# Routed experts on 131 tiles of chosen token rows in whole fp32 words, with the weights resident on chip and rows moved by indirect transfers

## The reference

```
x = x + xattn(layernorm(x), ctx, ctx)              # causal, 16 heads of 16
h = layernorm(x)                                   # (1600, 256)
scores = sigmoid(h @ gate_w.T)                     # (1600, 32)
sc     = scores + gate_bias
# 8 groups of 4 experts; the 4 groups with the best sum of their top two;
# in those the 8 best experts of sc; weights = scores of the 8, normalised, * 2.5
routed = einsum('tei,ehi->th', silu(h @ w_gate) * (h @ w_up) * combine, w_down)   # 32 experts, inner size 128
shared = (silu(h @ sh_gate.T) * (h @ sh_up.T)) @ sh_down.T                        # two more of size 128
out = x + routed + shared
```

## Time and profile before

| what | value |
|---|---|
| time, median of 3 runs | 690.34 us (689.27 to 690.46) |
| span of the profiled execution, first to last instruction | 687.6 us |
| TensorE busy, weight loads busy | 625.4 us, 569.0 us |
| VectorE, ScalarE, GpSimd busy | 559.5, 271.4, 249.4 us |
| granted TensorE clock, mean | 0.975 |
| moved by DMA | 61.66 MB, mean 90 GB/s |

### The profile page before, as it was taken

How to read it: one execution, slowest core, us unless ns; L and a number is a source line. 1 busy time by engine, 2 the same in 40 slices (tenths; PEclk the granted TensorE clock), 3 DMA queues, 4 the chain that set the end, 5 groups by cost and what they waited for, 6 DMA issues and landing times.

```text
span 687.6 us, 13004 instructions
## 1 busy us (share of the span) xinstructions
PE 625.4 (91%) x4232; PEld 569.0 (83%) x4232; DVE 559.5 (81%) x942; ACT 271.4 (39%) x590; POOL 249.4 (36%) x222
## 2 busy tenths in 40 slices
PE   3897999997589999999999999999999999999996
PEld 3885666664489898999999899999999999999995
DVE  5967999994748888888888888888888888888885
ACT  3444665652123333333333333333333333333331
POOL 6530334344013333333333333333333333333332
PEclk9999999998779999999999999999999999999998
DMA  6210000000123343433334343444343433333341
GB/s 192 80 59 1 2 2 3 2 2 0 49 74 94 98 133 97 122 111 113 120 101 131 95 125 109 131 120 125 102 131 94 130 104 119 115 102 132 95 123 49
DMA packets 33373, 61.66 MB, mean 90 GB/s; under 512 B 4008, under 2 KB 14768, under 8 KB 33348
## 3 DMA queue, kind: packets, MB, share of 16 engines
q1 hardware_dynamic: 33348, 61.31, 29.6%
HBM read 59.44 MB, written 1.86 MB: 89 GB/s over the span
## 4 chain that ended last, share of the span: by engine, by line
PE 76%; DVE 16%; issue 5%; ACT 1%; DMA 1%; POOL 0%; SPq 0%; DVEq 0%
PE ps L647 47%; PE ps L813 24%; DVE prob L498 4%; DVE rden L519 3%; DVE nm L489 2%; PE ps L834 2%; DVE st L509 1%; DVE xn L445 1%; DMA cst<-consts 1%; DVE ot L521 1%; DVE x_all L507 1%; PE ps L737 1%; PE ps L700 0%; PE ps L710 0%; PE ps L696 0%
## 5 line engine op out<-in xcount | busy, mean ns | idle before, releaser
L302 POOL TENSOR_TENSOR act<-act,cw 128x400 f32<-128x400 f32 x136 | 178.8, 1315 | 328.5 <-DVE act L595 328.5
L647 PE MATMUL ps<-h_hi_all,w_hi 128*128 128x400 f32 x544 | 189.0, 347 | 4.9 <-DVE w_lo L544 4.9
L393 ACT ACTIVATE act<-ps 128x400 f32<-128x400 f32 x136 | 68.5, 504 | 311.6 <-PE ps L647 311.6
L647 PE MATMUL ps<-h_lo_all,w_hi 128*128 128x400 f32 x544 | 188.9, 347 | 0.0
L647 PE MATMUL ps<-h_hi_all,w_lo 128*128 128x400 f32 x544 | 188.6, 347 | 0.0
L592 DVE SCALAR_TENSOR_TENSOR act<-act,ps 128x400 f32<-128x400 f32 x136 | 77.7, 571 | 83.5 <-ACT act L393 83.5
L813 PE MATMUL ps<-a_hi,w_hi 128*128 128x400 f32 x272 | 99.2, 365 | 19.5 <-issue 17.0
L647 PEld LDWEIGHTS ps<-h_hi_all,w_hi 128*128 128x128 f32 x544 | 103.2, 190 | 5.0 <-issue 5.0
L647 PEld LDWEIGHTS ps<-h_lo_all,w_hi 128*128 128x128 f32 x544 | 103.3, 190 | 0.0
L647 PEld LDWEIGHTS ps<-h_hi_all,w_lo 128*128 128x128 f32 x544 | 103.2, 190 | 0.0
L544 DVE TENSOR_TENSOR w_lo<-w_raw,w_hi 128x512 fp32r<-128x512 f32 x68 | 102.9, 1513 | 0.0
(11 more groups left out here) (118 smaller groups left out, 664.7 us busy)
## 6 DMA issues: line engine op xcount, KB each, us to landing
cw<-combine_rows SPq DMA_DIRECT2D x68, 400.0 KB, 4.0
w_raw<-w_exp SPq DMA_DIRECT2D x68, 256.0 KB, 3.9
w_raw<-w_exp SPq DMA_DIRECT2D x68, 128.0 KB, 2.0
x_all<-x SPq DMA_DIRECT2D x4, 400.0 KB
ctx_f<-ctx_t SPq DMA_DIRECT2D x4, 400.0 KB, 3.7
out_t<-y_out SPq DMA_DIRECT2D x8, 200.0 KB, 2.0
wa<-w_attn SPq DMA_DIRECT2D x4, 256.0 KB, 6.1
cst<-consts SPq DMA_DIRECT2D x1, 266.0 KB, 5.7
```

The lines of the kernel that those rows point to most:

```text
L302: pool.tensor_tensor(act[:, s, :], act[:, s, :], cw[:, (s // 2) % 2, (s % 2) * TG:(s % 2 + 1) * TG], ALU.mult).then_inc(weighted, 1)
L393: a.activation(act[:, s, :], ps[:, 4 + 2 * (s % 2), 0:TG], ACT.Tanh, scale=0.5).then_inc(tanh_e, 1)
L647: last = t.matmul(out, w, m, start=(i == 0), stop=(i == n - 1))
```

## The change

The routed experts are computed only for the rows that chose them. What is new, part by part:

- **Routing moves into the attention loop.** `route(p)` for two batches at a time runs on VectorE from the sixth turn of the loop on. Matmuls with a triangular matrix (`count`) count the rows that chose each expert so far, and `places` makes from it a row number in a DRAM table `chosen_rows`, in which every expert has 2048 places. The split of the normed rows into two parts goes away; the logits are plain fp32 matmuls, batch by batch.
- **Sends.** For each batch GpSimd issues 8 indirect transfers (`send`, L355): the r-th takes the batch's 100 records of 289 words (256 features, the row's number, 32 combine weights) to the places of each row's r-th expert; 128 transfers in all. 32 transfers of SyncE write 128 empty records behind each expert's last one (L274).
- **Weights resident.** All 32 experts' weights (12.6 MB) are loaded once into `w_all`: 9 experts early, 6 after the projections, 17 after the last `values`. The two shared experts are computed over all rows with plain fp32 matmuls (`shared_gate_up`, `shared_product`) and added to `x_all`, which starts the first of three sum tables in DRAM.
- **Tiles.** A table of 131 tiles of 128 rows (the most there can be: 12800 chosen rows plus 32 partly filled tiles) says for each its place and its expert. For each tile SyncE loads two registers and issues two transfers, the rows and their column of combine weights (L287 to L290); TensorE turns the rows (L946), loads a register with the place of the weights (L950), makes two fp32 matmuls for gate and up together (L955), turns the activations (L963) and makes one for down (L969), each 128 rows by 256 columns; ScalarE makes two copies and a tanh, VectorE three operations, GpSimd one indirect transfer that adds the 128 result rows in DRAM to one of the three sum tables by row number (L372). A tile's transfer waits until that of three tiles before has landed (`landed`).
- **End.** The three sum tables are fetched in four blocks, added on VectorE, turned on TensorE, copied and stored.

```diff
+NT = (T * TOPK + NE * (P - 1)) // P
...
+EARLY = 9
+MIDDLE = 6
+NSUM = 3
+NROW = 12
+NOUT = 5
...
+            def experts_load(first_one, end, arrived):
+                sp.dma_start(w_all[:, first_one:end, :], w_exp[2 + first_one:2 + end].rearrange("e p n -> p e n")).then_inc(arrived, 16)
+
...
+            sp.wait_ge(q_ready, KC * NG)
+            experts_load(EARLY, EARLY + MIDDLE, w_middle)
+            sp.wait_ge(pv_psum, NB)
+            for e in range(EARLY + MIDDLE, NE, 4):
+                experts_load(e, min(e + 4, NE), w_late)
...
+            sum_start(0)
+            sp.wait_ge(pads_at, 1)
+            for e in range(NE):
+                at = sp.value_load(pads[0:1, e:e + 1], min_val=0, max_val=PAD_ROWS - CAP + T)
+                sp.dma_start(recs[bass.ds(at, P), :], pad_rec[:]).then_inc(pads_out, 16)
...
+            sp.wait_ge(rows_out, 16 * NB * TOPK)
+            for i in range(NT):
+                b = i % NROW
+                if i >= NROW:
+                    n = (i - NROW) % NSUM
+                    sp.wait_ge(landed[n], times_landed(n, i - NROW + 1))
+                at = sp.value_load(table[0:1, 0, i:i + 1], min_val=0, max_val=PAD_ROWS)
+                e = sp.value_load(table[0:1, 1, i:i + 1], min_val=0, max_val=NE - 1)
+                sp.dma_start(rows[:, b, :], recs[bass.ds(at, P), 0:COMB]).then_inc(row_in[b], 16)
+                sp.dma_start(weight[:, b:b + 1], recs[bass.ds(at, P), bass.ds(e + COMB, 1)],
+                             allow_slow_non_contiguous=True).then_inc(row_in[b], 16)
...
+            for q, (j0, j1) in enumerate(BLOCKS):
+                for n in range(NSUM):
+                    sp.dma_start(fetched(n)[:, j0 * D:j1 * D].rearrange("p (j d) -> p j d", d=D),
+                                 sums[n][j0 * P:j1 * P, :].rearrange("(j p) d -> p j d", p=P)).then_inc(part_in[q], 16)
...
-                pool.tensor_copy(h_hi_all[:, :, batch_cols(B)], h_rows[:, B % 2]).then_inc(h_hi_ready, 1)
-                pool.wait_ge(h_hi_ready, B + 1)
-                pool.tensor_tensor(h_lo_all[:, :, batch_cols(B)], h_rows[:, B % 2], f(h_hi_all[:, :, batch_cols(B)]),
-                                   ALU.subtract).then_inc(h_lo_ready, 1)
...
+            def send(B):
...
+                pool.wait_ge(h1_ready, B + 1)
+                pool.wait_ge(comb_ready, B // 2 + 1)
+                pool.wait_ge(dest_ready, B // 2 + 1)
+                for r in range(TOPK):
+                    pool.indirect_dma_start(out=recs, out_offset=bass.IndirectOffsetOnAxis(ap=dest[:, B, r:r + 1], axis=0),
+                                            in_=rec[:, B, :], in_offset=None).then_inc(rows_out, 16)
...
-            def weigh(N, s, E, new_expert):
-                if new_expert:
-                    pool.wait_ge(cw_in[(s // 2) % 2], 16 * E)
-                pool.wait_ge(gated, N + 1)
-                pool.tensor_tensor(act[:, s, :], act[:, s, :], cw[:, (s // 2) % 2, (s % 2) * TG:(s % 2 + 1) * TG],
-                                   ALU.mult).then_inc(weighted, 1)
...
+                if B >= 5:
+                    send(B - 5)
+            for B in range(NB - 5, NB):
+                send(B)
...
+            for i in range(NT):
+                n = i % NSUM
+                pool.wait_ge(o_ready, i + 1)
+                if i >= NSUM:
+                    pool.wait_ge(landed[n], times_landed(n, i))
+                pool.indirect_dma_start(
+                    out=sums[n], out_offset=bass.IndirectOffsetOnAxis(ap=rows[:, i % NROW, TOKEN:TOKEN + 1].bitcast(U32), axis=0),
+                    in_=out_rows[:, i % NOUT, :], in_offset=None, compute_op=ALU.add).then_inc(landed[n], 16)
...
+            def rows_in(i):
...
+                a.activation(hx[:, i % 3, :], ps[:, i % 2, 0:D], ACT.Copy).then_inc(hx_ready, 1)
...
+            def gate(i):
...
+                a.activation(th[:, i % 2, :], ps[:, 2 + i % 2, 0:FI], ACT.Tanh, scale=0.5).then_inc(t_tanh, 1)
...
+            def acts_in(i):
...
+                a.activation(ax[:, i % 2, :], ps[:, 4 + i % 2, 0:P], ACT.Copy).then_inc(ax_ready, 1)
...
-            def split_gu(count, slot):
-                v.wait_ge(gu_hi, count)
-                v.tensor_tensor(w_lo[:, slot, 0:2 * D], w_raw[:, slot, 0:2 * D], f(w_hi[:, slot, 0:2 * D]),
-                                ALU.subtract).then_inc(gu_lo, 1)
...
+            def route(p):
+                two = slice(2 * p, 2 * p + 2)
+                v.wait_ge(tanh_ready, 2 * p + 2)
...
+                for b in range(2 * p, 2 * p + 2):
+                    then(v.tensor_tensor(so_far[:, b + 1, :], so_far[:, b, :], mask_e[:, b, :], ALU.add))
+                v.scalar_tensor_tensor(taken[:], rt[:, two, :], 1.0, mask_e[:, two, :], ALU.add, ALU.mult).then_inc(mask_ready, 1)
...
+            def places(p):
+                two = slice(2 * p, 2 * p + 2)
+                v.wait_ge(place_psum, p + 1)
+                then(v.tensor_tensor(place[:], ps[0:S, 6 if late_count(p) else 3, TG:TG + 2 * NE].rearrange("p (b e) -> p b e", e=NE), mask_e[:, two, :], ALU.mult))
+                then(*[v.max(first[:, b, :], place[:, b, :]) for b in range(2)])
+                v.tensor_scalar(dest[:, two, :], first[:], -1.0, None, ALU.add).then_inc(dest_ready, 1)
...
+            def gate(i):
+                n = i % 2
+                v.wait_ge(t_tanh, i + 1)
+                v.scalar_tensor_tensor(opened_t[:, n, :], th[:, n, :], 1.0, ps[:, 2 + n, 0:FI], ALU.add, ALU.mult).then_inc(t_open, 1)
+                v.wait_ge(t_open, i + 1)
+                if i >= 2:
+                    v.wait_ge(ax_psum, i - 1)
+                v.scalar_tensor_tensor(gated_t[:, n, :], opened_t[:, n, :], weight[:, i % NROW:i % NROW + 1], ps[:, 2 + n, FI:2 * FI],
+                                       ALU.mult, ALU.mult).then_inc(t_gated, 1)
+
+            def result(i):
+                v.wait_ge(t_down, i + 1)
+                if i >= NOUT:
+                    n = (i - NOUT) % NSUM
+                    v.wait_ge(landed[n], times_landed(n, i - NOUT + 1))
+                v.tensor_copy(out_rows[:, i % NOUT, :], ps[:, 6 + i % 2, 0:D]).then_inc(o_ready, 1)
+
+            for i in range(NT + 2):
...
-                for part_of in range(2):
-                    w = lambda a, k: a[:, slot, (2 * part_of + k) * P:(2 * part_of + k + 1) * P]
-                    last = product(ps[:, 4 + 2 * (s % 2) + part_of, 0:TG],
-                                   [(w(w_hi, k), w(w_lo, k), h_hi_all[:, k, col:col + TG], h_lo_all[:, k, col:col + TG])
-                                    for k in range(KC)])
-                last.then_inc(gu_psum, 1)
...
+            def weights(i):
+                off = place_of[i]
+                return w_all[:].rearrange("p e n -> p (e n)")[:, bass.ds(off, W)].rearrange("p (a n) -> p a n", n=P)
+
+            def rows_turned(i):
+                t.wait_ge(row_in[i % NROW], 32 * (i // NROW + 1))
+                if i >= 2:
+                    t.wait_ge(hx_ready, i - 1)
+                for k in range(KC):
+                    last = t.transpose(ps[:, i % 2, k * P:(k + 1) * P], rows[:, i % NROW, k * P:(k + 1) * P], ident)
+                last.then_inc(hx_psum, 1)
+
+            def gate_up(i):
+                place_of[i] = t.value_load(table[0:1, 2, i:i + 1], min_val=0, max_val=(NE - 1) * W)
+                t.wait_ge(hx_ready, i + 1)
+                if i >= 2:
+                    t.wait_ge(t_gated, i - 1)
+                for k in range(KC):
+                    last = t.matmul(ps[:, 2 + i % 2, 0:D].rearrange("p (a n) -> p a n", n=P), hx[:, i % 3, k * P:(k + 1) * P],
+                                    weights(i)[:, k:2 * KC:2, :], start=(k == 0), stop=(k == KC - 1))
+                last.then_inc(t_gu, 1)
+
+            def acts_turned(i):
+                t.wait_ge(t_gated, i + 1)
+                if i >= 2:
+                    t.wait_ge(ax_ready, i - 1)
+                t.transpose(ps[:, 4 + i % 2, 0:P], gated_t[:, i % 2, :], ident).then_inc(ax_psum, 1)
+
+            def down(i):
+                t.wait_ge(ax_ready, i + 1)
+                if i >= 2:
+                    t.wait_ge(o_ready, i - 1)
+                t.matmul(ps[:, 6 + i % 2, 0:D].rearrange("p (a n) -> p a n", n=P), ax[:, i % 2, :],
+                         weights(i)[:, 2 * KC:3 * KC, :], start=True, stop=True).then_inc(t_down, 1)
+
+            t.wait_ge(table_ready, 1)
+            t.wait_ge(sh_gated, 2 * NG)
+            t.wait_ge(sh_added, 2 * NG)
...
+            for i in range(NT + 2):
+                if i < NT:
+                    gate_up(i)
+                if i >= 2:
+                    down(i - 2)
+                if 1 <= i <= NT:
+                    acts_turned(i - 1)
+                if i + 2 < NT:
+                    rows_turned(i + 2)```

```

(5 more changed lines are left out.)

750 lines of the change are left out of this document (404 added, 346 removed).

## The result

The changed kernel takes **664.51 us** (median of 4 runs, 662.17 to 666.83) beside 690.40 us of the kernel before on the same chip (4 runs, 689.27 to 691.44). The ratio is 0.9627, with a 95% interval of 0.9600 to 0.9654: faster by 3.7%. Forecast were 639 us, with 570 to 770 as the range.

The account below looks back on a forecast made before the run. The prediction took GpSimd's sends to set the tile loop's start and TensorE to pace the tiles: 287 + 321 + 7 + 21 = 636 us of span, plus 2.7 gives 639 us; range 570 to 770.

Parts of the forecast that it names:

- First send: In attention: GpSimd's first indirect transfer of records was to begin at about 111 us.
- q: GpSimd's price for issuing one indirect transfer, taken as 1.2 us, between bounds of 0.56 and 2.84.
- SyncE waits for the last record, loads, fetches: 4 us.: Between the last send and the tile loop: SyncE's wait, register loads and fetch were to take 4 us.
- the 287 of the forecast: Start of the tile loop, forecast at 287 us; a start outside 260 to 310 would make the prediction wrong.
- Attention at 11.4 us a batch, set by GpSimd.: Attention under the sends: GpSimd's eight sends and a norm, 11.4 us a batch, set the pace against VectorE's 9.4.
- The longest is TensorE: 2.45 us a tile.: Tile loop: TensorE's 1.85 us plus a 0.60 register load sets the pace, 131 tiles in 321 us.
- Rival 2: Tile loop: slower register loads make SyncE the pace, 3.55 us a tile and 783 us in all; chance 0.10.
- L: Time a register load holds an engine's queue in the tile loop, taken as 0.60 us, between 0.05 and 2.0.
- The signs that the prediction named: Tile loop profile: a TensorE sequencer wait of about 0.6 us per tile for the forecast; waits for SyncE's rows otherwise.
- Landing, 5 us taken: Tile loop: an adding transfer lands in 5 us, 1.7 us a tile; it would decide only above 7.4 us.
- The end, 28 us.: After the tile loop: 7 us for the last tile, 16 for fetching three tables, 5 for the last block.
- Rival 4: Tile loop: TensorE falls to 1.2 GHz, 4.3 us a tile, 880 us; halfway, about 740; chance 0.06.

Follow-up runs that it names:

- experiment 9: Changed kernel with every fourth send made a second time into a table nobody reads, 32 more indirect transfers on GpSimd: 704.58 us.
- experiment 8: Changed kernel with the 16 norms of the second normalization moved from GpSimd to VectorE: 653.67 us.
- 10: Changed kernel with both: expert number worked out on SyncE without its register load, and norms on VectorE: 586.64 us.
- experiment 7: Changed kernel with one SyncE register load per tile (all weights from expert 0's column) and result transfers overwriting instead of adding: 578.95 us.
- experiment 3: Changed kernel with a third, unused register load on SyncE in each tile: 723.47 us.
- experiment 5: Changed kernel with the expert's number worked out from the row's number on SyncE instead of loaded: 601.57 us.
- experiment 6: Changed kernel with the expert's number worked out on SyncE and result transfers overwriting instead of adding: 588.08 us.

## Why the prediction was right, and where it was not

The direction, the structure (sends set the start, a latency and queue loop follows, an end of fetches) and the range held. The forecast was 25.5 us too low, and its main step gave the right number for a wrong reason, which is luck. By its own steps, in the span:

- **First send: 111 forecast, 112.4 measured.** Right: VectorE's 6.63 us turns and the small operations of `route` at 0.19 us.
- **"I take 1.2 us" for q.** Measured 0.99 of instruction plus 0.30 of gap, 1.29: short by 0.09, 12 us over 128 sends. The pass over as many words was a fair stand-in, but the gap behind each instruction was left out. The norms between cost 1.9 instead of 1.78, also by a gap. A pause was not foreseen at all: once in the sends GpSimd issues nothing for 5.6 us.

```profile
251.44 0.99 POOL L355 DMA_INDIRECT chosen_rows<-rec,dest  x1 [0.30 <-issue]
258.03 1.00 POOL L355 DMA_INDIRECT chosen_rows<-rec,dest  x1 [5.60 <-issue]
```

  That pause (3.5 to 6.8 us) is in the change and in all ten experiments, each time right behind the 93rd indirect transfer. In experiment 9, where the sends are more, the 93rd stands at an earlier batch, and the pause went with it; in 8 and 10 it came 12 to 15 us sooner, as the sends did. So it goes with the number of transfers, and neither with a place in the program nor with the time; what causes it stays open. Last send's end: 283 forecast, 302.0 + 1.29 = 303.3 measured.
- **"SyncE waits for the last record, loads, fetches: 4 us."** 8.3 measured, to TensorE's first operation on rows at 311.6. A send takes 5.6 us from its start to landing:

```profile
302.00 5.60 DMA chosen_rows<-rec,dest
```

  With this the loop starts 24.6 us later than the 287 of the forecast, and just outside the 260 to 310 that it named as the limit of being right: this term failed by its own test.
- **Attention at 11.4 us a batch, set by GpSimd.** Right in mechanism (12.5 measured); experiment 8 shows it, since VectorE took up 16 norms and the sends still ended earlier, and experiment 9, in which more sends ended later by their full price.
- **"The longest is TensorE: 2.45 us a tile."** This is the step that failed. The period, 2.41, is as forecast only because two errors met. TensorE's tile is 1.72 where rows are there, and at most 1.75 in experiment 7, not 1.85 + 0.60: the register load is done while earlier matmuls still run, so it lies beside them and not in series (the matmuls waited for the sequencer 5.6 us in all). SyncE was priced at 2.16 and set aside as the shorter; its step is 2.24, to which stray long loads and hand-overs add 0.17. The price of a load, taken as 0.60 from the nearest stall of a sequencer, was good: 0.55 in SyncE's step (experiment 3), though the load instruction itself is only 0.27. Rival 2 had the right engine. Its threshold, L = 0.9, was wrong by TensorE's side of the comparison. With TensorE at 1.75 and no L in it, SyncE's own term of 0.95 + 2L is the longer from L = 0.4 on, an estimate from experiment 7. The signs that the prediction named could not tell the two apart: a wait of about 0.6 us for TensorE's sequencer was there in 104 tiles (64.5 us, L955), as forecast, but on the weight loads, beside running matmuls; and a wait for rows was there too (21.7 us in the loop), the sign of rival 2.
- **Landing, 5 us taken, 3.9 measured**, 8.0 us of waits in the whole loop; VectorE and ScalarE as forecast far from pacing. That GpSimd's adding transfer costs the same q as a send was wrong: 1.54 + 0.30 beside 0.99 + 0.30. In the changed kernel it hides under SyncE; from experiment 5 on it counts.
- **The end, 28 us.** 131 periods from 311.6 end at 627.1, so it took 37.9. Last tile to landed: 11 instead of 7, with a copy, an adding transfer of 1.54 and 3.9 of landing behind the last matmul. Fetch, adds, turns, stores: 27 instead of 21.

In sum: start +24.6, loop -5.5, end +9.9, together 29.0, which is 665.0 less 636. The profiled execution lies 2.3 us above the median, and 1.8 rather than 2.7 us lie around the span; with 638.7 rounded to 639 that leaves the 25.5.

Rival 4, a fall of TensorE's clock in the tile loop, did not come: the granted clock there is 1.00, its higher level of 2.4 GHz, with TensorE busy 80 of 100 us in pieces. (Its case halfway, at 0.75, would be 287 + 131 x 3.07 + 31 = 720 us by its own terms, not 740.) It is under the sends that it fell, to 0.74 from 100 to 200 us, where TensorE was 76% busy and stood still up to 7.0 us for GpSimd's norm. That can't have moved the last send, as GpSimd waited for no engine but itself from the first send to the last. The Trainium skill ("TensorE: Matmul & The Clock Gate", part 1) says that activity alone lifts the throttled state; the trace agrees with that for these standstills, and shows that this loop with its short pauses keeps the full clock. Of the 1.3 us that the Trainium skill ("Runtime: NRT & Kernel Launch", "The launch sequence") gives for a load of registers from DRAM, no run here shows anything, as all loads come from SBUF; for these, at 0.27 us, it would have been far off.

How much of the possible gain the change as made gives away: 63 us to one register load per tile (664.5 - 601.6, experiment 5) and 11 to norms that share a queue with the sends (664.5 - 653.7, experiment 8). The version with both is 78 us faster than the changed kernel, 4 more than the two measured apart.

## What to carry to other kernels

Price a loop of small tiles for every queue, those that only load registers and hand over transfers included, and put a gap behind each instruction: here 0.55 us for a register load and 0.30 behind each of GpSimd's transfers were what counted, while all busy columns stood below 81%. Before naming one engine as the bound because its sum is the longest, ask of each term whether it is in series or beside the others on that engine; the sum that was second by 0.3 us was the true one. Then test it with a load added on either engine: one line each, and the answer was +59 us against none. Choose signs that only one of the two would leave. And read a period at the end of the pipeline as well as at its start: in experiment 5 the fetches came every 1.85 us and the results left every 1.88, and the later number named the bound.

## What the runs showed of the hardware that was not expected

- A register load from SBUF takes 0.27 us on SyncE and 0.30 on TensorE, but adds 0.55 to SyncE's step, and next to nothing to TensorE as long as it has slack.
- An indirect transfer from GpSimd takes it 0.96 us for 128 rows of 1 KB and 0.99 for 100 rows of 1.16 KB; adding makes the instruction 1.54 and the landing 3.9 instead of 2.5 us. About 0.30 us of idle time follows each. Adding also keeps the DMA engines busy: a share of 0.92 at 141 GB/s in experiment 5, of 0.52 at 144 GB/s without it in experiment 6.
- Right behind the 93rd indirect transfer GpSimd issued nothing for 3.5 to 6.8 us, in all 11 kernels of the change.
- The hand-over of a transfer on SyncE, 0.333 us as a rule, took up to 1.62 in the changed kernel, 9 times over 0.4 in its 262. Loads too were stray, up to 0.75. Together they made 0.07 to 0.18 us a tile in the kernels in which SyncE waited for no landed result. Their cause was not sought.
